# Latent attention of a fused two-layer block: queries projected two units earlier, another order of transfers, roots on GpSimd, expert weights split inside the head

## What is computed

```python
def _attention(x, Wq, Wkva, Wkvb, Wo):
    q = (x @ Wq).reshape(b, t, H, D).transpose(0, 2, 1, 3)       # 16 heads of 64
    ckv = x @ Wkva
    kv_latent, k_rope = (ckv[:, :, :R], ckv[:, :, R:])           # 32 and 32
    kv = (kv_latent @ Wkvb).reshape(b, t, H, NOPE).transpose(0, 2, 1, 3)
    q = jnp.concatenate([q_nope, _rope(q_rope)], axis=-1)
    k = jnp.concatenate([kv, _rope(k_rope)], axis=-1)
    att = jnp.einsum('bhqd,bhkd->bhqk', q, k) / jnp.sqrt(jnp.float32(D))
    att = jax.nn.softmax(jnp.where(mask, att, -jnp.inf), axis=-1)
    y = jnp.einsum('bhqk,bhkd->bhqd', att, v)
    return y.transpose(0, 2, 1, 3).reshape(b, t, H * D) @ Wo
x = x + _attention(_rmsnorm(x, w_ln1), Wq, Wkva, Wkvb, Wo)
return x + _moe(_rmsnorm(x, w_ln2), ...)                          # experts, routed and shared
```

## Time and profile before

| | us |
|---|---|
| median of 3 runs | 3424.22 |
| lowest, highest | 3422.98, 3429.47 |
| profiled execution | 3441.32 |
| span of its trace | 3439.3 |

### The profile page before, as it was taken

One profiled execution on the slowest core, in us unless ns is written; L12 is line 12 of the kernel. 1 busy time (PEld: TensorE's weight loads), 2 busy tenths in 40 slices (PEclk: granted clock), 3 DMA queues, 4 the chain that ended last, 5 costly groups with the idle time before them and its releaser, 6 DMA issues. The chain is left out here.

```text
span 3439.3 us, 44231 instructions
## 1 busy us (share of the span) xinstructions
PE 2789.8 (81%) x15344; PEld 2258.8 (66%) x15408; DVE 1863.7 (54%) x3464; ACT 1318.7 (38%) x1866; POOL 700.4 (20%) x804
## 2 busy tenths in 40 slices
PE   3879797937899899989989937999677772888897
PEld 3768595925677677767777726778554442777776
DVE  3546463625676676667666625555433334555555
ACT  0323242314565565556655523333222212332332
POOL 0010101032434344343432200101133330000000
PEclk8889898968999999999999968999888885999999
DMA  3000000024333433443343221111100002000000
GB/s 125 13 27 1 27 1 27 1 72 101 100 102 92 122 95 93 104 106 101 93 106 96 72 82 40 39 40 39 60 24 21 21 24 91 1 27 27 1 27 13
DMA packets 125119, 193.96 MB, mean 56 GB/s; under 512 B 36320, under 2 KB 94816, under 8 KB 118560
## 3 DMA queue, kind: packets, MB, share of 16 engines
q1 hardware_dynamic: 124896, 191.07, 19.4%
HBM read 121.69 MB, written 61.34 MB: 53 GB/s over the span
## 5 line engine op out<-in xcount | busy, mean ns | idle before, releaser
L1069 DVE TENSOR_TENSOR l_Plo<-l_s,l_Phi 128x1024 fp32r<-128x1024 f32 x288 | 352.2, 1223 | 202.5 <-ACT l_s L1277 200.2
L1057 DVE TENSOR_REDUCE l_negmax<-l_mx 128x1 f32<-128x512 f32 (+3 forms) x608 | 383.1, 652 | 129.4 <-PE l_mx L1396 129.1
L1273 ACT ACTIVATE l_Phi<-l_s 128x1024 fp32r<-128x1024 f32 x288 | 295.0, 1024 | 259.9 <-PE l_s L1416 259.1
L1396 PE MATMUL l_mx<-l_KK,l_QA 128*128 128x512 f32 (+3 forms) x768 | 286.9, 413 | 87.2 <-DMA l_QB<-l_qd 86.1
L1427 PE MATMUL l_o<-l_Phi,l_V 128*128 128x256 f32 x1152 | 318.3, 297 | 13.2 <-ACT l_Osb L1285 8.2
L1427 PE MATMUL l_o<-l_Plo,l_V 128*128 128x256 f32 x1152 | 311.1, 291 | 0.0
L1277 ACT ACTIVATE l_s<-l_s 128x1024 f32<-128x1024 f32 x288 | 294.4, 1022 | 0.0
L1414 PE MATMUL l_s<-l_QA,l_KK 128*128 128x512 f32 x576 | 282.7, 491 | 2.6 <-DVE l_Plo L1069 1.9
L1195 POOL TENSOR_TENSOR l_Y<-l_Osb,l_R 64x512 f32<-64x512 f32 x128 | 163.4, 1276 | 528.8 <-DMA l_R<-l_rd 524.0
L1427 PEld LDWEIGHTS l_o<-l_Phi,l_V 128*128 128x128 f32 x1152 | 228.7, 199 | 51.6 <-issue 39.4
L1941 ACT ACTIVATE m_hidhi<-m_results 128x512 fp32r<-128x512 f32 x168 | 106.3, 633 | 368.0 <-DVE m_results L1847 368.0
(11 more groups left out here) (274 smaller groups left out, 6276.4 us busy)
## 6 DMA issues: line engine op xcount, KB each, us to landing
l_qd<-l_qs SPq DMA_DIRECT2D x256, 128.0 KB, 2.4
l_QA<-l_qd SPq DMA_DIRECT2D x64, 512.0 KB, 4.9
l_QB<-l_qd SPq DMA_DIRECT2D x64, 256.0 KB, 5.7
l_R<-l_rd SPq DMA_DIRECT2D x128, 128.0 KB, 3.0
m_xb<-xs SPq DMA_DIRECT2D x10, 1024.0 KB, 4.9
l_rps<-l_rp SPq DMA_DIRECT2D x128, 64.0 KB, 2.4
m_ub<-u SPq DMA_DIRECT2D x5, 1024.0 KB, 6.7
w_xb<-in_x SPq DMA_DIRECT2D x4, 1024.0 KB, 5.4
```

What stands on the lines that cost most here:

```text
L1057: v.tensor_reduce(negmax[:, n % 2, at + h0:at + h1], piece_of(number, chunk), AX.X, ALU.max, negate=True).then_inc(reduced, 1)
L1069: v.tensor_tensor(Plo[:, s % 3].rearrange("p u h q -> p (u h q)"), S2[s % 2][:, :], Phi[:, s % 3].rearrange("p u h q -> p (u h q)").bitcas ...
L1273: a.activation(Phi[:, s % 3].rearrange("p u h q -> p (u h q)"), S2[s % 2][:, :], ACT.Exp, scale=L_D ** -0.5).then_inc(exped, 1)
L1396: mm = pe.matmul(bank[:, h - h0, :], QA[:, n % 4, h, t, :], KK[:, b % 2, k0 * P:k1 * P], start=not diagonal, stop=(h == h1 - 1), skip_grou ...
```

## The change

1. **Query projection.** `query`, `query_high` and `query_low` are done for step m + 4 in unit 8 of step m, in place of step m + 3 in unit 1. These are two units earlier against the use of the tile, which doesn't move. The steps begin at -4 in place of -3.
2. **Other uses of `PJ`.** `max_turn` with its copy moves from i = 4 to i = 3, `out` from 5 and 7 to 4 and 6, `add_out` from 6 and 8 to 5 and 7, the pieces one unit up. `rope_queries` moves from i = 3 to 1, `normal_out` from 7 to 6, `query_low` to i = 0. `join_max` stays at i = 3.
3. **Order on SyncE.** The swap comes first in a step. The store of the queries and the broadcast of `R` come before the store of the maxima's row. The loads of `QA` and `QB` come before the load of that row. The load of the sums and `load(b)` come last.
4. **Roots.** GpSimd adds EPS and raises to the power -0.5 (two operations on 128x8 elements); ScalarE's `root` and VectorE's `inverse_std` go.
5. **Experts.** In the head of the first sequence the splits are interleaved with `ahead(0, 0)`: the high parts before the copies of u = 0, after those of u = 0 and after those of u = 2; the low parts after the normalization, after the first L1751 and after the third.

The diff, cut to its core (what SyncE moves is shown by the rows above):

```diff
@@ class LatentPlan
-    FIRST, LAST = -3, STEPS + 2
+    FIRST, LAST = -4, STEPS + 2
-    PIECE_AT = {(8, 7): 0, (9, 5): 1, (9, 7): 2, (11, 5): 3, (11, 7): 4, (12, 5): 5, (12, 7): 6}
+    PIECE_AT = {(8, 6): 0, (9, 4): 1, (9, 6): 2, (11, 4): 3, (11, 6): 4, (12, 4): 5, (12, 6): 6}
@@ TensorE
-                if i == 1 and L.is_step(m + 3):
-                    query(m + 3)
-                if i == 4 and L.is_step(m + 1):
+                if i == 3 and L.is_step(m + 1):
                     max_turn(m + 1)
-                if i in (5, 7) and m % 4 == 2 and m >= 6:
-                    out((m - 6) // 4, (i - 5) // 2)
+                if i in (4, 6) and m % 4 == 2 and m >= 6:
+                    out((m - 6) // 4, (i - 4) // 2)
+                if i == 8 and L.is_step(m + 4):
+                    query(m + 4)
@@ VectorE
-                if i == 2 and L.is_step(m + 3):
+                if i == 0 and L.is_step(m + 3):
                     query_low(m + 3)
-                    if (ls, i) == (5, 4):
-                        inverse_std(2 * b + 1)
-                    if (ls, i) == (8, 4):
-                        inverse_std(2 * b + 2)
@@ GpSimd
+            def inverse_root(b, n):
+                ...
+                g.tensor_scalar(std[:, :], mv[:, :, 1], EPS, None, ALU.add).then_inc(std_ready, 1)
+                g.wait_ge(std_ready, 2 * b + n + 1)
+                g.tensor_tensor(rstd[:, :], std[:, :], minus_half[:, :], ALU.pow).then_inc(rstd_ready, 1)
-                if i == 3 and L.is_step(m + 3):
+                if i == 1 and L.is_step(m + 3):
                     rope_queries(m + 3)
-                if i == 7 and L.is_step(m - 2):
+                if i == 6 and L.is_step(m - 2):
                     normal_out(m - 2)
+                    if (ls, i) in ((5, 2), (8, 2)):
+                        inverse_root(b, (ls - 5) // 3)
@@ ScalarE
-                if i == 1 and L.is_step(m + 3):
-                    query_high(m + 3)
-                if i == 4 and L.is_step(m + 1):
+                if i == 3 and L.is_step(m + 1):
                     max_row(m + 1)
+                if i == 8 and L.is_step(m + 4):
+                    query_high(m + 4)
-                    if (ls, i) == (5, 2):
-                        root(b, 0)
-                    if (ls, i) == (8, 2):
-                        root(b, 1)
@@ experts
+        SPLIT_AT = (LOAD + 3, LOAD + 4, LOAD + 6)
@@ experts, VectorE
-            for _ in ahead(0, 0):
-                pass
-            for n, (hi, lo) in enumerate(splits):
-                v.wait_ge(split_hi, n + 1)
-                v.tensor_tensor(lo, staged[n % 2][:, 0:NT * C], hi.bitcast(F32), ALU.subtract)\
-                    .then_inc(split_lo, 1)
+            for step, _ in enumerate(ahead(0, 0)):
+                if step in SPLIT_AT:
+                    n = SPLIT_AT.index(step)
+                    ...
@@ experts, ScalarE
-            for _ in ahead(0, 0):
-                pass
-            for n, (hi, _) in enumerate(splits):
-                a.wait_ge(staging[n % 2], (n // 2 + 1) * 16)
-                a.activation(hi, staged[n % 2][:, 0:NT * C], ACT.Copy).then_inc(split_hi, 1)
+            for step, _ in enumerate(ahead(0, 0)):
+                if step - LOAD - 1 in (0, 1, 3):
+                    n = (step - LOAD) // 2
+                    a.wait_ge(staging[n % 2], (n // 2 + 1) * 16)
+                    a.activation(splits[n][0], staged[n % 2][:, 0:NT * C], ACT.Copy).then_inc(split_hi, 1)
```

More of the change, by code:

```diff
@@ L717, in bank_work @@
     def bank_work(self, m, i):
-        if i == 1 and self.is_step(m + 3):
-            yield "query", m + 3
-        if i == 4 and self.is_step(m + 1):
+        if i == 3 and self.is_step(m + 1):
             yield "max", m + 1
-        if i in (5, 7) and m % 4 == 2 and m >= 6:
-            yield "out", ((m - 6) // 4, (i - 5) // 2)
+        if i in (4, 6) and m % 4 == 2 and m >= 6:
+            yield "out", ((m - 6) // 4, (i - 4) // 2)
+        if i == 8 and self.is_step(m + 4):
+            yield "query", m + 4
         piece = self.piece(m, i)
@@ L910, in _ @@
                 ahead = L.is_step(m) and b < B
+                if L.is_step(d):
+                    sp.wait_ge(qact, 2 * d + 1)
+                    if d >= 2:
+                        sp.wait_ge(roped, d - 1)
+                    for odd in range(2):
+                        sp.dma_start(rps[odd:P:2, d % 2], rp[1 - odd:P:2, d % 2]).then_inc(qswap[d % 2], 16)
                 if L.is_step(r):
@@ L921, in _ @@
                 if L.is_step(d):
-                    sp.wait_ge(qact, 2 * d + 1)
+                    sp.wait_ge(roped, d + 1)
+                    sp.wait_ge(freed_v, L.after("query", d))
                     if d >= 2:
-                        sp.wait_ge(roped, d - 1)
+                        sp.wait_ge(qready[(d - 2) % 4], 32 * ((d - 2) // 4 + 1))
+                    for h in range(4):
+                        sp.dma_start(QD[d % 2, :, :, h, :].rearrange("c i x -> i c x"),
+                                     qs[32 * h:32 * h + 32, d % 2].bitcast(F32).rearrange("i a c x -> i (a c) x"))\
+                            .then_inc(qstored[d % 2], 16)
+                if L.is_step(r):
+                    sp.wait_ge(rstored[r % 2], 16 * (r // 2 + 1))
+                    if r >= 2:
+                        sp.wait_ge(normal, 2 * (r - 1))
                     for odd in range(2):
-                        sp.dma_start(rps[odd:P:2, d % 2], rp[1 - odd:P:2, d % 2]).then_inc(qswap[d % 2], 16)
+                        sp.dma_start(R[64 * odd:64 * odd + 64, r % 2].rearrange("p t q -> p (t q)"),
+                                     RD[r % 2, odd].partition_broadcast(64)).then_inc(rready[r % 2], 16)
                 if L.is_step(n):
@@ L977, in _ @@
                         .then_inc(qready[d % 4], 16)
+                if L.is_step(n):
+                    sp.wait_ge(mstored[n % 2], 16 * (n // 2 + 1))
+                    if n >= 4:
+                        sp.wait_ge(scored, UNITS * (n - 3))
+                    sp.dma_start(QB[64:65, n % 4].bitcast(F32),
+                                 MD[n % 2:n % 2 + 1].rearrange("o (t h) q -> o h t q", t=2))\
+                        .then_inc(mready[n % 2], 16)
+                if L.is_step(c):
+                    sp.wait_ge(sstored[c % 2], 32 * (c // 2 + 1))
+                    if c >= 2:
+                        sp.wait_ge(inverse, c - 1)
+                    sp.dma_start(sums[:, c % 2, :], SD[c % 2].rearrange("o t (a e) -> (o t a) e", e=8))\
+                        .then_inc(sready[c % 2], 16)
+                if ahead and ls == 3:
+                    load(b)
                 if ahead and ls == 13:
```

67 lines of the change are left out of this document (19 added, 48 removed).

## The result

The changed kernel takes 3451.8 us in the median of 6 runs (3442.3 to 3465.3), the kernel before 3429.3 us in the median of its 6 runs on the same chip. The ratio is 1.0074, with a 95% interval of 1.0051 to 1.0098: **slower by 0.7%**, 22 us. That lies inside the range of the prediction (3388 to 3458), but 25 us above its point, and in the range of its case "the row of maxima sets the pace" (3445 to 3466). The profiled execution took 3449.9 us, its span is 3448.1.

The account below looks back on a forecast made before the run. It took TensorE, busy 1088 of 1187 us, as the latent loop's bound. Terms -68.0 - 18 + 83 + 24 - 4.5 + 8 - 21.8 = +2.7 gave 3444 us by the profiled execution, 3427 by the median; 8 in 10: 3388 to 3458.

Parts of the forecast that it names:

- the row of maxima sets the pace: Rival in the latent loop: projection-to-row chain of 18.0 us or more shows in short steps; 3466, milder 3445; chance 0.26.
- The tile's waits: Latent loop: all 68.0 us of TensorE's waits for the query tile at the first chunk of `maximum` go; -68.0 us.
- The clock: Latent loop: part of the 119 us run at 1.2 GHz comes back; -18 us, with 0 and 40 as ends.
- The turn of the maxima: `max_turn` in unit 3: TensorE waits for `join_max`, 1.6 us in 32 odd steps, 1.0 in 32 even; +83 us.
- The row behind the tile: The maxima's row, loaded behind `QA` and `QB`, comes late in some 20 short steps at 1.2 us; +24 us.
- Roots and small terms: Roots off ScalarE -6, one projection less -1.5, projection waiting in unit 8 in three steps +3; together -4.5 us.
- The start: Start of the pipeline: the third query tile's store and loads go ahead of the first maxima's row; +8 us.
- The experts: Heads of both expert stages: first products come 10.5 and 11.3 us earlier; together -21.8 us, good to 3.
- From the profile to the median: Last step: the sum made on the profiled execution, 3441.3 us, scaled to the median of runs, 0.5% below it.

Follow-up runs that it names:

- e1: The kernel before with only the change to the experts' split: 3406.6 us against 3426.4, ratio 0.9943.
- e5: e4 with the load of the sums too moved ahead of the query tile's two loads: 3385.4 us, ratio to before 0.9871.
- e7: e6 with the transposition of the maxima back in unit 4, output products and pieces with it: 3428.7 us, ratio to before 0.9995.
- e4: The changed kernel with the maxima's row load ahead of the query tile's loads and the transposition back in unit 4: 3425.3 us, ratio to before 0.9987.
- e6: The changed kernel with all of SyncE's program in the order of before, transposition still in unit 3: 3406.0 us, ratio to before 0.9936.
- e8: The changed kernel with only the loads of the maxima's row and the sums moved ahead of the query tile's loads: 3412.4 us, ratio to before 0.9945.
- e2: The changed kernel with only the load of the maxima's row moved ahead of the query tile's two loads: 3446.0 us, ratio to before 1.0059.
- e9: The kernel before with only the roots done by GpSimd's power: 3423.3 us against 3428.5, ratio 0.9982.
- e3: The changed kernel with the transposition of the maxima back in unit 4, output products and pieces with it: 3427.3 us, ratio to before 1.0000.
- e11: e5 with `query_low` on VectorE moved to unit 1, behind the reductions of unit 0: 3378.7 us, ratio to before 0.9845.

## Why the prediction was right or wrong

The predicted time was 25 us too low. It fell in the range of a case that had a chance of 0.26, but that case's mechanism came true only in part: the row cost 11 us more than the forecast has and not 21, and a wait that no case names cost about twice that. So the hit within the range is partly luck. Step by step, from the profiled executions:

- **The tile's waits** (-68.0): right. The line is gone.
- **The clock** (-18): the direction was right. TensorE's busy time in the loop fell by 8.8 us, and e1 says that 7.0 of that is the difference between two executions of the same loop. So the term is worth little in after. It is there in e5, where the long waits are gone: 1064.8 us busy at 0.98.
- **The turn of the maxima** (+83): the mechanism was right, the size too high by more than half. The waits are 37.9 us in 48 places, 1.34 in step 45 and 1.5 at most, where the prediction had 1.6 and 1.0 in all 64. In even steps it is 9.7 us in all and not 32, since TensorE is late itself there, by the wait for the reductions that comes just ahead. The joined line and the reductions together grew by 58.5 us.
- **The row behind the tile** (+24): right in kind, too low. The waits in the loop rose by 35, in 31 places by 1.2 us each. The row takes 4.9 us from issue to first use in step 45, as the earlier trace rows had it. That it lies written for 3.3 us ahead of its store had been worked into the chain, and the chain's length was right: where TensorE waited, 17.5 us in the median from the end of the projection to the first score, against 17.2. What failed is the count: the prediction had a wait in every second short step at most, and there was one in 27 of the 36.
- **The reductions** (no term of their own): +23.5 us. This is the step that is missing. The prediction knew that unit 2 follows unit 1 at once and drew the consequence for the turn, where it allowed "two more hundred nanoseconds" for a reduction in unit 2. It didn't ask what the projection had hidden between the two units: in unit 2 of odd steps before waits for no reduction, and every kernel with the projection in unit 8 waits there, 11.7 us in after, 14.9 in e7 and 30.0 at most (e4). In unit 3 of even steps the tile's wait had covered the same lateness: e7, whose tile is late again, waits there for reductions for 0.8 us, after for 13.9.
- **The sums** (not in the sum either): the prediction names the load of the maxima's row as the one thing that moves behind the tile. The sums' load moved there too: in before it was issued ahead of `R` and the tile, in after it is the last of SP's round. In after itself no wait of TensorE for a reduction follows from it through VectorE's work without a gap, and with the sums early (e6, e8) the reductions still cost 30.7 and 38.3 us. Its price shows in e2 and e4, once the row no longer holds TensorE up: 44 and 63 us of waits, and 40 us of time from e4 to e5.
- **Roots and small terms** (-4.5): the roots' own -6 agrees with e9 (-5, uncertain). Missed was that the pieces, one unit earlier, find VectorE's normalization unfinished: +11.6 us in two lines where +3 was allowed.
- **The start** (+8): 6.7 us, the first score at 809.59 in place of 802.86.
- **The experts** (-21.8): 10.6 and 11.7 us, 22.3 in all; right.
- **From the profile to the median.** The terms' sum was +2.7 and the profiled executions differ by +8.6, which looks close. The medians differ by 22. The profiled execution of before lies 12 us above that kernel's median, and the prediction took such an excess as a factor for both. But the profiled execution of after lies 2 us below its own. The excess was not a property of the kernel: e1 has the same loop in 1178.1 us. Against that loop after's is longer by 35.9 us, where the prediction had +16.5.

The Trainium skill (DMA: Bandwidth & Descriptors, Queues, rings and completion order) states that each DMA engine takes one issuing engine's descriptors in the order of its ring. It also says that transfers of one issuing engine need not complete in the order of their issue, so by itself it doesn't forbid that a small load lands ahead of a large one. The traces show it for small transfers behind this tile: in before none of 60 stores of `rd`, and in after and e4 none of 60 loads of the sums each, landed ahead of the last `QB` issued in front of it. The median of the sums' load from issue to landing is 2.2 us before, 4.0 in after, 4.8 in e4, where they stand right behind `QB`, and 1.7 in e5, where they are ahead of `QA`.

## What to carry to other kernels

When a large transfer is moved ahead in a queue, list every small one that it passes, and for each the engine that waits for it and what stands behind that wait. Here a load of 4 KB that no TensorE instruction reads cost nothing that shows as long as another wait lay over it, and 40 us (e4 to e5) when that one had been removed. When work is moved out of a gap, ask what the gap had hidden: the projection's old place between units 1 and 2 was the time in which VectorE's reductions caught up. A wait that leaves a trace's list has not left the kernel: e2 and e3 each took away some 40 us of waits and gained 6 and 25. And an order of work and the unit in which its parts are made can't be judged one by one; the transposition in unit 4 is worth 0.7% with one order of the queue and costs 0.6% with another.

## What the runs showed of the hardware

- GpSimd's power on 128x8 numbers takes 1.67 us each, more than twice one product of 128x256 on the same engine (0.74 us). The prediction's bound of 1 us, taken from the nearest row, was too low.
- The runs of one kernel scatter by up to 1%: 31 runs of before on one chip went from 3408.9 to 3443.4 us. Two profiled executions of the same loop differ by 9.2 us, 7.0 of them TensorE's busy time, with a mean granted clock of 0.95 and 0.96. A difference of 0.2% can't be read from one profile of each kernel.
- The same matmuls, but for one projection, took TensorE 1064.2 to 1068.7 us at a mean granted clock of 0.98 in the loops of e5, e6, e8 and e11, and 1080.0 to 1092.9 us at 0.95 to 0.97 in those of before, e7, after, e2, e3 and e4. So 10 to 25 us can go with the clock beside what the list of waits has. The tile's waits alone don't decide it: e3 has none of them and the highest busy time. Nor does idle time in all: after idles for 133.9 us and is busy for 1080.0, before idles for 98.5 and is busy for 1088.8. What does decide it isn't shown by any run here.
